# Row maxima of causal attention: the mask added on VectorE, the products made for two heads at once in 64-row halves

## The reference

```
x = x + layernorm(attention(layernorm(x)))     # 16 heads of 64, rotary, causal
x = x + layernorm(ffn(layernorm(x)))           # linear, SwiGLU, mixture of 8 experts, linear, SwiGLU
attention: scores = q k^T / 8; scores = where(causal, scores, -inf); probs = softmax(scores); out = probs v; out @ wo^T
```

## Time and profile before

| | |
|---|---|
| median of 3 runs | 1261.14 us (1259.26 to 1264.67) |
| the profiled execution's own time | 1261.32 us |
| its span (first to last instruction) | 1259.3 us |
| mean granted TensorE clock | 0.975 |
| PE busy | 1144.7 us, 91% |
| DVE busy | 983.3 us, 78% |
| ACT busy | 956.5 us, 76% |
| POOL busy | 947.3 us, 75% |
| one slot of the attention (start of one L742 to the next, 770.80 to 828.70) | 57.9 us |
| attention, then FFN | about 0 to 1000 us, 1000 to 1259 us |

### The profile page before, as it was taken

How to read it: one execution, slowest core, us unless ns; L and a number is a source line. 1 busy time by engine, 2 the same in 40 slices (tenths; PEclk the granted TensorE clock), 3 DMA queues, 4 the chain that set the end, 5 groups by cost and what they waited for, 6 DMA issues and landing times. The chain is left out here.

```text
span 1259.3 us, 34888 instructions
## 1 busy us (share of the span) xinstructions
PE 1144.7 (91%) x13543; PEld 788.8 (63%) x13543; DVE 983.3 (78%) x2220; ACT 956.5 (76%) x2193; POOL 947.3 (75%) x984
## 2 busy tenths in 40 slices
PE   4689999999999999999999999999999598999996
PEld 1256676676767676767667676767777454566553
DVE  7798777787868797878778787979674559867987
ACT  3667888878787878787887879787979665766574
POOL 3578889889888989898988889898767475334463
PEclk8699999999999999999999999999999899999998
DMA  6652425243351515152515334251602100000011
GB/s 201 147 135 52 123 65 129 60 118 82 89 127 43 133 38 136 37 134 69 129 49 128 83 87 118 53 135 35 153 2 65 51 2 1 1 1 1 2 35 34
DMA packets 50660, 97.03 MB, mean 77 GB/s; under 512 B 6720, under 2 KB 23360, under 8 KB 48448
## 3 DMA queue, kind: packets, MB, share of 16 engines
q1 hardware_dynamic: 50496, 94.81, 30.2%
HBM read 58.47 MB, written 34.60 MB: 74 GB/s over the span
## 5 line engine op out<-in xcount | busy, mean ns | idle before, releaser
L807 POOL TENSOR_TENSOR Plo<-P,Phi 128x512 f16<-128x512 f32 (+3 forms) x640 | 538.3, 866 | 129.2 <-ACT P L498 128.6
L495 ACT ACTIVATE Phi<-psS 128x512 f16<-128x512 f32 (+3 forms) x768 | 384.0, 500 | 149.5 <-PE psS L353 105.9
L498 ACT ACTIVATE P<-psS 128x512 f32<-128x512 f32 (+3 forms) x640 | 307.0, 480 | 0.0
L347 PE MATMUL psS<-Q,K 128*128 128x512 f16 (+3 forms) x768 | 252.0, 328 | 40.5 <-DVE Plo L654 37.1
L374 PE MATMUL psO<-V,Plo 128*128 128x65 f16 x2304 | 288.7, 194 | 0.0
L370 PE MATMUL psO<-V,Phi 128*128 128x65 f16 x2304 | 287.5, 192 | 0.0
L372 PE MATMUL psO<-V,Phi 128*128 128x64 f16 x2304 | 286.6, 192 | 0.0
L703 DVE TENSOR_REDUCE pmax<-psX 128x1 f32<-128x512 f32 x384 | 252.9, 684 | 23.0 <-PE psX L434 14.3
L370 PEld LDWEIGHTS psO<-V,Phi 128*128 128x128 f16 x2304 | 219.5, 98 | 56.6 <-issue 0.4
L350 PE MATMUL psS<-Q,K 65*128 65x512 f16 (+3 forms) x768 | 252.2, 328 | 0.0
L434 PE MATMUL psX<-K,Q 128*128 128x512 f16 (+4 forms) x768 | 227.5, 332 | 11.7 <-DMA Q<-HL 3.8
(11 more groups left out here) (200 smaller groups left out, 2161.1 us busy)
## 6 DMA issues: line engine op xcount, KB each, us to landing
K<-k_way SPq DMA_DIRECT2D x48, 512.0 KB, 7.0
k_way<-HL SPq DMA_DIRECT2D x64, 256.0 KB, 3.7
q_way<-HL SPq DMA_DIRECT2D x60, 256.0 KB, 3.7
Q<-q_way SPq DMA_DIRECT2D x60, 256.0 KB, 7.1
Q<-q_way SPq DMA_DIRECT2D x15, 512.0 KB, 11.9
out<-y SPq DMA_DIRECT2D x8, 256.0 KB, 2.2
y<-in_x SPq DMA_DIRECT2D x3, 512.0 KB, 10.8
hn<-in_x SPq DMA_DIRECT2D x3, 512.0 KB, 5.5
```

Source lines behind the costliest of these rows:

```text
L347: nc.tensor.matmul(out, M.K1[:, p, h, j * P:(j + 1) * P], M.Q1[:, p, h, c:c + w], start=True, stop=False)
L495: nc.scalar.activation(M.Phi[:, U % NP_, 0:w], X, ACT.Exp, scale=SCALE)
L498: nc.scalar.activation(full, X, ACT.Exp, scale=SCALE).then_inc(S.exp_done, 1)
L807: nc.gpsimd.tensor_tensor(M.Plo[:, U % NP_, 0:w], M.P32[:, U % NP_, 0:w], M.Phi[:, U % NP_, 0:w], ALU.subtract).then_inc(S.lo_pool, 1)
```

## The change

Three things are changed, in "mx" alone.

1. The mask products of "mx" (L438) go. Where a segment ends on the diagonal, DVE takes its maximum with tensor_tensor_reduce: it adds a bfloat16 mask from SBUF (zero, with the causal triangle in its last 128 columns), writes the sum back over the segment in PSUM, and puts the running maximum straight into `rmax`. The other four segments of a head are reduced by tensor_reduce, also into `rmax`. So there are 12 DVE instructions for a head (4 tensor_reduce of 512, 8 tensor_tensor_reduce of 512, 512, 384, 384, 256, 256, 128 and 128), where there were nine tensor_reduce; where a row of tiles has two segments, the second starts from the value that the first left. `pmix`, `pmax`, `join_head` and `join_max` go.
2. From slot 0 on, the products of heads 2i and 2i + 1 are made together (`both_heads`), with 64 rows each: the even head in rows 0 to 63, the odd head in rows 64 to 127, each into its own `psX` bank. They multiply only the high halves of keys and queries. For this the odd heads' `K1` is loaded with its halves exchanged, in two DMAs instead of a share of one: SP issues ten loads of `K1` and `Q1` a slot instead of six, five of them counted by `near_in[0]` (same bytes).
3. Both items of a pair stand at one step, so 18 pairs stand at steps 8 to 38. PE waits for both banks of a pair before the first product. `MAXB` is put in another order, and "mt" goes from step 43 to 42.

```diff
-MAXB = [[(2, 0, 3), (0, 0, 1)], [(6, 4, 3), (4, 4, 1)], [(1, 0, 2), (5, 4, 2)],
-        [(3, 0, 4)], [(4, 0, 4)], [(5, 0, 4)], [(6, 0, 4)], [(7, 0, 4)], [(7, 4, 4)]]
+MAXB = [[(4, 0, 4)], [(5, 0, 4)], [(6, 0, 4)], [(7, 0, 4)], [(7, 4, 4)],
+        [(3, 0, 4)], [(2, 0, 3), (0, 0, 1)], [(6, 4, 3), (4, 4, 1)], [(1, 0, 2), (5, 4, 2)]]
+PAIRED = range(len(MAXB))
-MX_FIRST, MX_LAST, JOIN_STEP, MT_STEP = 8, 39, 40, 43
+MX_FIRST, MX_LAST, MT_STEP = 8, 39, 42
...
+                for i in range(GH * len(MAXB)):
+                    pair, k, odd = i // 2 // len(MAXB), i // 2 % len(MAXB), i % 2
+                    own = i - odd if k in PAIRED else i
+                    put(s, first + own * (last - first) // (GH * len(MAXB) - 1), ("mx", 2 * pair + odd, k))
...
+            def both_heads(item):
+                s, kind, h, k = item
+                p = (s + 1) % 2
+                other = (s, kind, h + 1, k)
+                if number[other] >= NAUX:
+                    pe.wait_ge(S.aux_free[bank(other)], number[other] // NAUX)
+                c = 0
+                for t, j, n in MAXB[k]:
+                    for x, low in ((item, 0), (other, HD)):
+                        mm = nc.tensor.matmul(M.psX[:, bank(x), c:c + n * P],
+                                              M.Q1[low:low + HD, p, x[2], t * P:(t + 1) * P],
+                                              M.K1[low:low + HD, p, x[2], j * P:(j + n) * P], start=True, stop=True)
+                        if (t, j, n) == MAXB[k][-1]:
+                            mm.then_inc(S.aux_ready, 1)
+                    c += n * P
...
-                        if diagonal:
-                            mm = nc.tensor.matmul(X[:, c - P:c], M.ident16[:], M.maskN[:], start=False, stop=True)
...
-                    if k < NMIX:
-                        nc.vector.tensor_reduce(M.pmix[:, h, k, :], X.rearrange("p (j i) -> p j i", i=P), AX.X,
-                                                ALU.max).then_inc(free(item), 1)
-                    else:
-                        t, j, _ = MAXB[k][0]
-                        nc.vector.tensor_reduce(M.pmax[:, int(j > 0), h, t:t + 1], X, AX.X,
-                                                ALU.max).then_inc(free(item), 1)
+                    for t, j, n in MAXB[k]:
+                        own = M.rmax[:, h * TT + t:h * TT + t + 1]
+                        part = X[:, c:c + n * P]
+                        c += n * P
+                        if j + n - 1 < t:
+                            last = nc.vector.tensor_reduce(own, part, AX.X, ALU.max)
+                        else:
+                            if j > 0:
+                                taken(dve, (s, "mx", h, MAXB.index([(t, 0, 4)])))
+                            last = nc.vector.tensor_tensor_reduce(
+                                out=part, in0=part, in1=M.mask[:, BANK - n * P:BANK], scale=1.0,
+                                scalar=own if j > 0 else LOWEST, op0=ALU.add, op1=ALU.max, accum_out=own)
+                    last.then_inc(free(item), 1)
...
-                    sp.dma_start(M.K1[:, p, h], krows[:, h]).then_inc(S.near_in[i], 16)
+                    sp.dma_start(M.K1[:, p, 2 * i], krows[:, 2 * i]).then_inc(S.near_in[i], 16)
+                    sp.dma_start(M.K1[0:HD, p, 2 * i + 1], krows[HD:P, 2 * i + 1]).then_inc(S.near_in[i], 16)
+                    sp.dma_start(M.K1[HD:P, p, 2 * i + 1], krows[0:HD, 2 * i + 1]).then_inc(S.near_in[i], 16)
```

More of the change, by code:

```diff
@@ L130, in plan @@
                     put(s, V_STEPS[tp], ("v", tp))
[L131 to L134, removed]
+            if s < 0:
+                for h in range(GH):
+                    slot, u = MX_FIRST_GROUP[h]
+                    for k in range(len(MAXB)):
                         at.setdefault((slot, u + k), []).append((s, "mx", h, k))
-                    else:
-                        first, last = MX_SECOND if s == 0 else (MX_FIRST, MX_LAST)
-                        i = h * len(MAXB) + k
-                        put(s, first + i * (last - first) // (GH * len(MAXB) - 1), ("mx", h, k))
+            else:
+                first, last = MX_SECOND if s == 0 else (MX_FIRST, MX_LAST)
+                for i in range(GH * len(MAXB)):
+                    pair, k, odd = i // 2 // len(MAXB), i // 2 % len(MAXB), i % 2
+                    own = i - odd if k in PAIRED else i
+                    put(s, first + own * (last - first) // (GH * len(MAXB) - 1), ("mx", 2 * pair + odd, k))
             if s < 0:
@@ L352, in scores @@
                 if diagonal:
-                    mm = nc.tensor.matmul(out[:, 0:P], M.ident16[:], M.maskT[:], start=False, stop=True)
+                    mm = nc.tensor.matmul(out[:, 0:P], M.mask[:, BANK - P:BANK], M.ident16[:], start=False, stop=True)
                 mm.then_inc(S.scores_ready, 1)
@@ L428, in side @@
                         else:
-                            pe.wait_ge(S.near_in[h // 2], 48 * (s + 1))
+                            pe.wait_ge(S.near_in[h // 2], 80 * (s + 1))
+                    if s >= 0 and k in PAIRED:
+                        if h % 2 == 0:
+                            both_heads(item)
+                        return
                     c = 0
@@ L432, in side @@
                     for t, j, n in MAXB[k]:
-                        diagonal = j + n - 1 == t
                         mm = nc.tensor.matmul(X[:, c:c + n * P], M.Q1[0:rows, p, h, t * P:(t + 1) * P],
-                                              M.K1[0:rows, p, h, j * P:(j + n) * P], start=True, stop=not diagonal)
+                                              M.K1[0:rows, p, h, j * P:(j + n) * P], start=True, stop=True)
                         c += n * P
-                        if diagonal:
-                            mm = nc.tensor.matmul(X[:, c - P:c], M.ident16[:], M.maskN[:], start=False, stop=True)
                 elif kind == "mt":
@@ L441, in side @@
                         h = a[0]
-                        pe.wait_ge(S.row_max, h + 1)
+                        taken(pe, (s, "mx", h, len(MAXB) - 1))
                         mm = nc.tensor.transpose(X[0:TT, 0:P], M.rmax[:, h * TT:(h + 1) * TT], M.ident[:])
                     else:
-                        pe.wait_ge(S.row_max, s + 1 + GH)
+                        taken(pe, (s, "mx", GH - 1, len(MAXB) - 1))
                         mm = nc.tensor.transpose(X[0:GH * TT, 0:P], M.rmax[:], M.ident[:])
@@ L714, in side @@
                         nc.vector.tensor_tensor(y, X, y, ALU.add).then_inc(free(item), 1)
[L716 to L743, removed]
             def y_statistics(batch):
@@ L832, in _ @@
             nc.gpsimd.memset(M.ident16[:], 0.0)
-            nc.gpsimd.memset(M.maskT[:], 0.0)
-            nc.gpsimd.memset(M.maskN[:], 0.0).then_inc(S.consts, 1)
+            nc.gpsimd.memset(M.mask[:], 0.0).then_inc(S.consts, 1)
             pool.wait_ge(S.consts, 1)
@@ L838, in _ @@
                                         pattern=[[-1, P]], channel_multiplier=1)
-            nc.gpsimd.affine_select(out=M.maskT[:], in_=M.maskT[:], compare_op=ALU.is_ge, fill=NEG, base=0,
-                                    pattern=[[1, P]], channel_multiplier=-1)
-            nc.gpsimd.affine_select(out=M.maskN[:], in_=M.maskN[:], compare_op=ALU.is_ge,
+            diagonal = M.mask[:, BANK - P:BANK]
+            nc.gpsimd.affine_select(out=diagonal, in_=diagonal, compare_op=ALU.is_ge,
                                     fill=NEG, base=0, pattern=[[-1, P]], channel_multiplier=1).then_inc(S.consts, 1)
@@ L920, in send @@
                     for i in range(2):
-                        sp.wait_ge(S.near_in[i], 48 * (s + 1))
+                        sp.wait_ge(S.near_in[i], 80 * (s + 1))
                     sp.wait_ge(S.far_in, 32 * (s + 1))
@@ L996, in phase_attention @@
         M.ident16 = sb(stack, "ident16", [P, P], BF16)
-        M.maskT = sb(stack, "maskT", [P, P], BF16)
-        M.maskN = sb(stack, "maskN", [P, P], BF16)
+        M.mask = sb(stack, "mask", [P, BANK], BF16)
         M.x_tiles = I["x"].rearrange("b (t p) d -> p (b t) d", p=P)
```

24 lines of the change are left out of this document (10 added, 14 removed).

## The result

The changed kernel takes 1293.5 us (median of 4 runs, 1291.18 to 1299.5) against 1260.2 us: ratio 1.027, 95% interval 1.0247 to 1.0292. It is 33 us slower, where 1244 us were forecast and 1281 was the upper end of the range.

What follows compares the result with a forecast made beforehand. PE was taken to bound the 44 us of a slot with row maxima, ACT and POOL the other 14. 1261.3 - 15.4 (fourteen slots) - 2.0 (slot 14) gave 1244 us; forecast band 1232 to 1254, full range 1215 to 1281.

Steps and rivals of the forecast that it cites:

- What bounds the kernel: In a slot's 44 us with row maxima PE sets the time, busy 42.9 us, with DVE 4 us behind.
- PE, before and after: PE's work on maxima in a slot: 9.4 us becomes 6.7, a saving of 2.7 us (1.6 to 3.6).
- The switch: PE's change between 64 and 128 rows: 0.08 us each, 36 a slot, 2.9 us (2.0 to 4.0).
- DVE: DVE's work on maxima in a slot: 22.8 us becomes 25.0 (22.5 to 27.5), 2.2 us more.
- The eight hand-outs: Handing out DVE's accumulator after each tensor_tensor_reduce: half of 0.72 us taken, 0.36 us a head.
- the fixed part: Cost of a tensor_tensor_reduce on DVE beyond its elements: 0.057 us without a column operand, 0.124 with one.
- The stretch after: A slot's 44 us with row maxima become 42.9, 1.1 us less in fourteen slots, as DVE passes PE.
- the bank wait: Before each pair PE waits for the first bank of the pair before: 0.3 us a pair, 1284 us; chance 0.13.
- the other rivals: PE and DVE cheap, 1221 us (0.17); DVE dear, 1279 (0.12); pairs not overlapping, 1278 (0.10); no visible change, 1259 (0.13).
- Slot 14: Slot without "qk" work: PE's saving comes through but for what ACT makes of it, -2.0 us.
- Slot -1: First head's PE time shrinks but the DVE that follows has more to do: nothing, 1 us either way.
- Edits at nothing: Ten loads, about 1 us later under 1.6 us of cover, earlier "mt", `MAXB` order and mask as weights cost nothing.

## Why the prediction was wrong

**What bounds the kernel.** Half right. PE had the most to do, but its work could not be counted one to one: switches of 7.6 us a slot cost 3.3. And DVE mattered before it was full: shortening its maxima, without pairs, gave 37 us (1255.3 to 1218.3) though DVE was busy 40.6 of 43.9 us. Two engines that wait for each other over three banks both set the time; that reading fits both runs but was not tested by itself.

**PE, before and after.** The columns and the overlap are right. The switch was taken as 0.08 us and is 0.1, as at 1.2 GHz: at most 3.8 us a slot, not 2.9. By that PE's saving is 1.8 us, not 2.7, inside its bounds. That the drain exists the Trainium skill states (TensorEngine Tiling (Array Packing), Key Properties), and that row groups run side by side too (TensorE: Matmul & The Clock Gate, Part 3: Packing small matmuls); this trace agrees with both, 0.1 us and 0.32 us for two times 512 columns.

**DVE.** Right: 3.79 us a head were forecast, and the starts give 3.6 (one of 512 at 0.63 and one at 0.68, 384 at 0.49 and 0.54, 256 at 0.37 and 0.40, 128 at 0.25 and 0.27). The eight hand-outs, put at 0.36 us a head, took nothing from start to start; the fixed part was a little larger instead. Without pairs the rest of the change (mask, join, `MAXB`, the order of heads and "mt" together) is worth 4 to 5 us, about 0.35%, in two runs.

**The stretch after: the step that failed.** "I charge 0.2 us a slot beyond today's 0.7". PE's idle time before side work (the waits for `psX` banks, two of which are in the earlier trace rows) went from 4.7 us to 66 us (55.6 + 6.4 + 3.0 and 1.1 of a smaller group) in 810 us, that is from 0.3 to 4.9 us a slot. The account closes: with the idle time before scores (33.7, then 21.2 us) PE idles 2.8 us a slot before and 6.5 after; 3.7 more, less the 1.8 of work saved, is 1.9 us, and the slots grew by 2.1 on average. I had forecast 1.1 less. This is the bank wait, the rival to which 0.13 was given. Its price, 0.3 us a pair or 5.4 us a slot, was nearly right. That its 1284 us came within 10 us is partly luck: the sum lacked the dearer switches and PE's other idle time of 1.1 us a stretch, which the other rivals had, and it lacked the shorter waits before scores. Its reason was too narrow: it named the first bank of the pair before, and a third of the waits and more are for banks of "qk" and V. What I argued against it, that PE seldom waited for a reduce before, was no evidence: every item needs the bank of the item three before it. With one item at a step, PE asks for it a step later; with pairs, the second item asks at the step of the first, and the holder is then still at work.

**Slot 14 and the start.** Slot 14 was put at -2.0 us, for PE's saving should come through there; it took 2.0 us more (54.1 against 52.1), and without pairs 51.6. Slot -1 was put at nothing, with 1 us either way; together with slot 0, whose maxima are in pairs and which was to gain 1.1 us, it took 3.2 us more.

**Where the 33 us are.** The change without pairs -5; two items at one step +27; both banks before the first product, segments in turns, +15; overlap less switches -4 (within the noise): together +33. These are differences of single edits in this order; what DVE's dearer maxima cost (13 us in the paired kernel, not measured without pairs) lies inside them and is not split off.

**Edits at nothing.** The ten loads: right without pairs (1255.6 against 1255.3). "mt" and the order of `MAXB` were not tried alone.

## What to carry to other kernels

Before handing out buffers in twos, count the buffers: with three in turn, a pair leaves one for the work that it follows, and the length that counts is that of any holder, not of the work that was changed. Packing two small products into the array saves their columns and pays two switches: with 0.2 us for both, a pair of 512 columns saves nothing. By that sum packed products want to be placed many in a row, which was not tried. The part of the change that takes work off PE without a pair, the mask on DVE and no join, is faster than both kernels, if by little: 0.9965 and 0.9968 of the one before in two runs.

## What the runs showed of the hardware

The switch between 64 and 128 rows costs 0.1 us at 2.4 GHz, about the 0.11 of 1.2 GHz: in these rows it does not shrink with the clock. The accumulator's hand-out on DVE has a row of 0.14 us, but the next instruction starts with it. An addition and maximum in one DVE instruction that writes back to PSUM takes 0.63 to 0.68 us for 512 elements, against 0.60 for a plain two-input operation.
